# Moving the third layer's expert-weight preparation behind its attention, on four banks, and the fourth layer's weight loads behind the first eight blocks

## What is computed

```python
x = x + _L2_xattn_ref(_layernorm(x), ctx_768, ...)   # one head of 128, 8 batches
x = x + _L2_ffn_ref(_layernorm(x), gate_w, w1, w3, w2)

def _L2_ffn_ref(x, gate_w, w1, w3, w2):              # HIDDEN = 352, 8 experts, TOP_K = 2
    scores = softmax(xf @ gate_w.T)
    expert_weights, expert_indices = top_k(scores, 2)
    ...
    for e in range(8):
        xe = where(flat_idx == e, x_rep, 0.0)
        h = silu(xe @ w1[e].T) * (xe @ w3[e].T)
        y = y + where(flat_idx == e, h @ w2[e].T, 0.0)
```

## Time and profile before

| | us |
|---|---|
| three runs | 1746.24, 1752.26, 1752.90 |
| median | 1752.26 |
| the profiled execution, its own time | 1750.34 |
| its span | 1748.6 |
| between keys/values and token tail of the second layer | 1002.5 to 1024.3 |
| token tail, boundary | 1024.3 to 1057.2 |
| attention of the third layer | 1057.2 to 1128.2 |
| until the first block | 1128.2 to 1144.65 |
| blocks of the third layer | 1144.65 to 1268 |

### The profile page before, as it was taken

One profiled execution on the slowest core, in us unless ns is written; L12 is line 12 of the kernel. 1 busy time (PEld: TensorE's weight loads), 2 busy tenths in 40 slices (PEclk: granted clock), 3 DMA queues, 4 the chain that ended last, 5 costly groups with the idle time before them and its releaser, 6 DMA issues.

```text
span 1748.6 us, 38773 instructions
## 1 busy us (share of the span) xinstructions
PE 1428.4 (82%) x12639; PEld 1092.7 (62%) x12639; DVE 1140.9 (65%) x3004; ACT 808.6 (46%) x1792; POOL 428.2 (24%) x749
## 2 busy tenths in 40 slices
PE   4989999988999778998966836468847988988977
PEld 2667777766666557777745624356635676766765
DVE  4767777776666658888765445633345888878861
ACT  1655555554343256666642223122215666666632
POOL 2000000011100033333222236733341222222221
PEclk9999999998999899999978957589968999999989
DMA  8999000000000030000001120111110000000000
GB/s 232 264 131 83 0 0 0 0 1 1 1 1 0 0 112 5 3 3 6 3 4 43 45 68 7 38 46 45 37 52 1 2 0 0 0 0 0 1 1 25
DMA packets 109760, 55.07 MB, mean 31 GB/s; under 512 B 44593, under 2 KB 102578, under 8 KB 109474
## 3 DMA queue, kind: packets, MB, share of 16 engines
q1 hardware_dynamic: 106146, 46.53, 14.0%
q0 software_dynamic: 3520, 7.31, 1.3%
HBM read 27.09 MB, written 26.74 MB: 31 GB/s over the span
## 4 chain that ended last, share of the span: by engine, by line
PE 58%; DVE 19%; issue 9%; POOL 5%; ACT 4%; SPq 2%; POOLq 1%; DVEq 1%; DMA 1%; ACTq 0%
PE bank L1579 49%; PE bank L1583 10%; DVE PTs L2315 4%; DVE negm L2301 2%; DVE negm L2304 2%; DVE VxF L787 1%; SPq L883 1%; ACT Pm L1419 1%; POOL token_rows_by_expert L1108 1%; ACT PTs L1377 1%; DVE st L2102 1%; POOLq L657 1%; ACT Qz L1377 1%; POOL yn L1315 1%; DVE rk L2465 1%
## 5 line engine op out<-in xcount | busy, mean ns | idle before, releaser
L1419 ACT ACTIVATE Pm<-bank,negm 128x256 f32<-128x256 f32 x784 | 321.6, 472 | 343.6 <-DVE negm L2304 251.5
L1579 PE MATMUL bank<-kT,Qz 64*128 64x256 f32 (+2 forms) x1568 | 305.1, 409 | 9.7 <-ACT Pm L1419 7.2
L1583 PE MATMUL bank<-ident,Pm 128*128 128x128 f32 x1568 | 233.6, 285 | 58.1 <-DVE PTs L2315 54.6
L2315 DVE TENSOR_TENSOR PTs<-bank,PTs 128x512 f16<-128x512 f32 x384 | 251.2, 682 | 33.3 <-ACT PTs L1377 32.2
L1583 PEld LDWEIGHTS bank<-ident,Pm 128*128 128x128 f32 x1568 | 177.7, 144 | 133.0 <-issue 89.0
L1579 PEld LDWEIGHTS bank<-kT,Qz 64*128 64x128 f32 (+1 forms) x1568 | 186.8, 192 | 84.3 <-issue 49.6
L2304 DVE TENSOR_REDUCE negm<-bank 128x2 f32<-128x512 f32 x264 | 176.3, 686 | 79.5 <-PE bank L1579 75.6
L1377 ACT ACTIVATE PTs<-bank 128x512 f16<-128x512 f32 (+1 forms) x388 | 218.3, 603 | 3.4 <-PE bank L1583 3.2
L1579 PEld LDWEIGHTS bank<-VxF,PTs 128*128 128x128 f16 (+1 forms) x4672 | 186.9, 101 | 11.2 <-DVE PTs L2315 2.8
L1579 PE MATMUL bank<-VxF,PTs 128*128 128x65 f16 (+3 forms) x4672 | 191.2, 190 | 1.9 <-DVE PTs L2315 1.9
L1579 PE MATMUL bank<-Qz,R 128*128 128x128 f16 x978 | 92.1, 230 | 23.1 <-ACT Qz L1377 13.9
(11 more groups left out here) (312 smaller groups left out, 2148.8 us busy)
## 6 DMA issues: line engine op xcount, KB each, us to landing
token_rows_by_expert<-trash SPq DMA_DIRECT2D x10, 1782.0 KB, 17.6
Qz<-token_rows_by_expert SPq DMA_DIRECT2D x62, 66.0 KB, 1.8
Qz<-expert_rows_by_token SPq DMA_DIRECT2D x12, 256.0 KB, 3.2
R<-in_L_ffn_ew SPq DMA_DIRECT2D x2, 1024.0 KB, 7.2
R<-in_L_ffn_w SPq DMA_DIRECT2D x1, 2048.0 KB, 9.5
R<-in_L_xattn_Wkv SPq DMA_DIRECT2D x2, 768.0 KB, 6.5
R<-in_L_ffn_w SPq DMA_DIRECT2D x1, 1408.0 KB, 12.0
R<-in_L_xattn_Wq SPq DMA_DIRECT2D x2, 512.0 KB, 3.9
```

Source lines behind the costliest of these rows:

```text
L1419: last = act.activation(Pm[:, k % 4, qt * S:(qt + 1) * S], bank[k % 2][:, qt * S:(qt + 1) * S], ACT.Exp, bias=negm[:, k % 4, qt:qt + 1])
L1579: return pe.matmul(o, l, r, start=start, stop=stop)
L1583: return pe.transpose(o, i, ident[0:n, 0:n])
L2315: dve.tensor_tensor(PTl[:, k % 4, :], bank[2 + k % 2][:, :], PTh[:, k % 4, :], ALU.subtract).then_inc(s.pt[1].sem, 1)
```

## The change

Three things are moved.

- The preparation of the third layer's expert weights leaves `early(ATT[2])`. A new `routed_weights()` on PE, ACT and DVE does the same 20 fills after the third layer's attention: on PE ahead of the first block's transposes, on ACT after the exponentials of the routing weights, on DVE after the block table. The fills use the four banks 0 to 3 in turn instead of banks 6 and 7, so four can be under way.
- SP issues the ten `l3` loads from within the third layer's block rows, after eight blocks' loads and ahead of the ninth.
- What works on those weights follows: `prep3_part(i - 5)` in place of `prep3_part(i)`, POOL's two maxima before block 15's store in place of block 10's, and POOL waits for `prep[2].filled` ahead of its clears.

```diff
+            def last_layer_weights():
+                sp.wait_ge(prep[2].filled, len(PREP2_UP) + len(PREP2))
+                load("l3", L3Wq, a["L3_xattn_Wq"])
+                load("l3", L3Wkv, a["L3_xattn_Wkv"])
...
+                load("l3", Bpr, a["L3_ffn_B_proj"])
...
                 for i in range(nb):
+                    if F.n == 2 and i == RING:
+                        last_layer_weights()
                     at = sp.value_load(rowoff[0:1, i:i + 1], min_val=0, max_val=8 * REGION + 6 * P)
                     if i >= RING:
...
-            sp.wait_ge(prep[2].filled, len(PREP2_UP) + len(PREP2))
-            load("l3", L3Wq, a["L3_xattn_Wq"])
...
                     if F.n == 1 and i == 14:
                         largest(2)
-                    if F.n == 2 and i == 10:
+                    if F.n == 2 and i == 15:
                         pool.wait_ge(vmax3_rows, 1)
...
+                    pool.wait_ge(prep[2].filled, len(PREP2_UP) + len(PREP2))
                     pool.memset(NVflat, 0.0)
...
+                            prep_evac(move, kind, k, bank_of(n)).then_inc(prep[3].act, 1)
+
+            def routed_weights():
+                act.wait_ge(up_scale, 3)
+                for n, (kind, k) in enumerate(PREP2_UP):
+                    need(act, prep[2].filled, n + 1)
+                    w = 512 if k < 5 else 256
+                    move(l2_parts(kind, k * 512, w)[0], bank[n % 4][:, 0:w], upscale[:, 2:3]).then_inc(prep2_high, 1)
+                for n, (kind, k) in enumerate(PREP2, len(PREP2_UP)):
+                    if n % 2 == 0:
+                        need(act, prep[2].filled, n + 1)
+                        prep_evac(move, kind, k, bank[n % 4]).then_inc(prep[2].act, 1)
 
...
                     act.activation(c_e, c_gd, ACT.Exp).then_inc(r.exped.sem, 1)
+                    routed_weights()
...
+            def routed_weights():
+                s, r = att_s[2], prep[2]
+                loaded(pe, "l2f")
+                need(pe, s.exp, ATT[2].nh)
+                need(pe, s.pt[0], ATT[2].nh // 2)
+                need(pe, s.pt[1], ATT[2].nh // 2)
+                nu = len(PREP2_UP)
+                for n, (kind, k) in enumerate(PREP2_UP + PREP2):
+                    if 4 <= n < nu + 4:
+                        pe.wait_ge(prep2_low, n - 3)
+                    elif n >= 4:
+                        pe.wait_ge(r.dve if n % 2 else r.act, (n - nu) // 2 - 1)
+                    prep_fill(kind, k, bank[n % 4]).then_inc(r.filled, 1)
+                need(pe, r.act, len(PREP2) // 2)
+                need(pe, r.dve, len(PREP2) // 2)
...
             def routed_by_token(F):
 
                 s, r = ffn_s[F.n], routed_s[F.n]
+                if F.n == 2:
+                    routed_weights()
...
+                for n, (kind, k) in enumerate(PREP2_UP):
+                    dve.wait_ge(prep2_high, n + 1)
+                    w = 512 if k < 5 else 256
+                    high, low = l2_parts(kind, k * 512, w)
+                    dve.scalar_tensor_tensor(low, bank[n % 4][:, 0:w], upscale[:, 2:3], high,
+                                             ALU.mult, ALU.subtract).then_inc(prep2_low, 1)
+                for n, (kind, k) in enumerate(PREP2, len(PREP2_UP)):
...
+                        need(dve, prep[2].filled, n + 1)
+                        prep_evac(move, kind, k, bank[n % 4]).then_inc(prep[2].dve, 1)
...
                 dve.tensor_tensor(rowoff[:, 0:nb], c_ro[:, 0:nb], step128[:, 0:nb], ALU.add).then_inc(r.table.sem, 1)
+                if F.n == 2:
+                    routed_weights()
...
                     if F.n == 2:
-                        prep3_part(i)
+                        prep3_part(i - 5)
```

More of the change, by code:

```diff
@@ L1387, in early @@
                 attention(A, ("early",))
-                if A.n in prep:
-                    r = prep[A.n]
-                    before = 0
-                    if A.n == 2:
-                        before = len(PREP2_UP)
-                        act.wait_ge(up_scale, 3)
-                        for n, (kind, k) in enumerate(PREP2_UP):
-                            need(act, r.filled, n + 1)
-                            w = 512 if k < 5 else 256
-                            move(l2_parts(kind, k * 512, w)[0], bank_of(n)[:, 0:w],
-                                 upscale[:, 2:3]).then_inc(prep2_high, 1)
-                    for n, (kind, k) in enumerate(PREP2 if A.n == 2 else PREP3):
-                        if n % 2 == 0:
-                            need(act, r.filled, before + n + 1)
-                            prep_evac(move, kind, k, bank_of(n)).then_inc(r.act, 1)
+                if A.n == 3:
+                    for n, (kind, k) in enumerate(PREP3):
+                        if n % 2 == 0:
+                            need(act, prep[3].filled, n + 1)
+                            prep_evac(move, kind, k, bank_of(n)).then_inc(prep[3].act, 1)
[9 more added lines that the diff above has]
+                        prep_evac(move, kind, k, bank[n % 4]).then_inc(prep[2].act, 1)
             def attention(A, early=None):
@@ L1648, in early @@
                 attention(A, ("early",))
-                if A.n in prep:
-                    r = prep[A.n]
+                if A.n == 3:
+                    r = prep[3]
                     need(pe, att_s[A.n].ring.act, (sum(step[0] in FILLS for step in att_early(A)) + 1) // 2)
                     need(pe, att_s[A.n].ring.dve, sum(step[0] in FILLS for step in att_early(A)) // 2)
-                    if A.n == 2:
-                        loaded(pe, "l2f")
-                    if A.n == 2:
-                        for n, (kind, k) in enumerate(PREP2_UP):
-                            if n >= 2:
-                                pe.wait_ge(prep2_low, n - 1)
-                            prep_fill(kind, k, bank_of(n)).then_inc(r.filled, 1)
-                        pe.wait_ge(prep2_low, len(PREP2_UP))
-                    for n, (kind, k) in enumerate(PREP2 if A.n == 2 else PREP3):
+                    for n, (kind, k) in enumerate(PREP3):
                         if n >= 2:
@@ L1877, in ffn_end @@
                 A = ATT[F.n + 1]
-                if A.n not in prep:
+                if A.n != 3:
                     need(pe, att_s[A.n].ring.act, (sum(step[0] in FILLS for step in att_early(A)) + 1) // 2)
@@ L2222, in early @@
                 attention(A, ("early",))
-                if A.n in prep:
-                    evacuate_prep(A)
+                if A.n == 3:
+                    evacuate_prep3()
             def values_scale_and_ones(A):
@@ L2240, in values_scale_and_ones, with routed_weights, evacuate_prep3 @@
                     last.then_inc(ones_set, 1)
-            def evacuate_prep(A):
-                r = prep[A.n]
-                before = 0
-                if A.n == 2:
-                    before = len(PREP2_UP)
-                    for n, (kind, k) in enumerate(PREP2_UP):
-                        dve.wait_ge(prep2_high, n + 1)
-                        w = 512 if k < 5 else 256
-                        high, low = l2_parts(kind, k * 512, w)
-                        dve.scalar_tensor_tensor(low, bank_of(n)[:, 0:w], upscale[:, 2:3], high,
-                                                 ALU.mult, ALU.subtract).then_inc(prep2_low, 1)
-                for n, (kind, k) in enumerate(PREP2 if A.n == 2 else PREP3):
-                    if n % 2:
-                        need(dve, r.filled, before + n + 1)
-                        prep_evac(move, kind, k, bank_of(n)).then_inc(r.dve, 1)
+            def routed_weights():
+                for n, (kind, k) in enumerate(PREP2_UP):
[5 more added lines that the diff above has]
+                for n, (kind, k) in enumerate(PREP2, len(PREP2_UP)):
+                    if n % 2:
+                        need(dve, prep[2].filled, n + 1)
+                        prep_evac(move, kind, k, bank[n % 4]).then_inc(prep[2].dve, 1)
+            def evacuate_prep3():
+                for n, (kind, k) in enumerate(PREP3):
+                    if n % 2:
+                        need(dve, prep[3].filled, n + 1)
+                        prep_evac(move, kind, k, bank_of(n)).then_inc(prep[3].dve, 1)
             def attention(A, early=None):
```

20 lines of the change are left out of this document (9 added, 11 removed).

## The result

The changed kernel took 1731.53 us (median of four runs, 1729.05 to 1736.52) beside 1752.49 us for the kernel before; the ratio is 0.9892, with an interval of 0.9861 to 0.9923. The forecast was 1731, with a range of 1724 to 1739. The profiled execution of the changed kernel is the slowest of its four, 1736.52 us with a span of 1734.8.

The account below looks back on a forecast made before the run. Between the layers no engine was busy throughout and the preparation stood alone; after the attention PE and ACT idled awaiting POOL's scatters. -21.8 + 1.5 - 0.8 = -21.1 from 1750.3 gave 1729.2, as a median 1731 us, range 1724 to 1739.

Parts of the forecast that it names:

- The 21.8 us taken away: Between second and third layer: without the 20 fills DVE goes straight from the last value copy to the token tail, -21.8 us.
- GpSimd's delay moves along: In the token tail: the 6.9 us before POOL's first instruction follows its trigger, so it does not swallow the gain.
- The preparation after the attention, +1.5 us: Between attention and first block: fills end at 1146.2, midway between both clock cases, against 1144.65, adding 1.5 us.
- case of full clock: Preparation after the attention: DVE sets the pace, the end is at 1144.3, before the first block's rows, cost 0.
- case of half clock: Preparation after the attention: PE sets the pace, the end is at 1147.9, 3.3 us late.
- The first blocks' 0.8 us: First blocks' up projections: a PE that has just worked runs them at a higher clock, -0.8 us.
- The loads at no cost: Ten `l3` loads among the block rows: landed by 1165.1, ninth block wanted at about 1167, cost 0.
- rival 1: Preparation after the attention stays at half clock and sticks out: -18.5 us in all, 1734 us; chance 0.17.
- rival 2: Ninth block's rows come late because the ten loads take twice as long: some 7 us, 1738 us; chance 0.06.
- rival 3: The attention's first 26 us stay at clock 0.50, at most 16 us more, 1747 us; chance 0.07.
- rival 4: The clock stays low through the third layer's blocks, 32 us more, 1763 us, slower; chance 0.04.
- rival 5: More than forecast: preparation at cost 0, blocks' 1.0 us back, up to 2 us from the tail, 1727 to 1729; chance 0.06.

Follow-up runs that it names:

- pool_ready: Changed kernel plus one small GpSimd tensor_scalar behind the last scatter of both routed layers, ahead of the wait for statistics: 1714.72 us, ratio 0.9802 to the kernel before.
- two_banks: Changed kernel with the preparation behind the attention on two banks in place of four: 1736.74 us, ratio 0.9918 to the kernel before.
- again: Changed kernel timed a second time, nothing edited: 1726.92 us, ratio 0.9862 to the kernel before.
- bridge: Changed kernel with 12 more transposes on TensorE behind the preparation, into an unread bank: 1728.5 us, ratio 0.9876 to the kernel before.
- bridge_long: Changed kernel with 32 more transposes on TensorE behind the preparation, into an unread bank: 1728.12 us, ratio 0.9875 to the kernel before.
- loads_first: Changed kernel with the ten loads issued ahead of the third layer's block rows, not after eight blocks' loads: 1737.54 us, ratio 0.9922 to the kernel before.
- old_place_four: Kernel before with the preparation and ten loads at their old place, but using four banks: 1741.53 us, ratio 0.9947 to the kernel before.
- pool_done: pool_ready with GpSimd's drain behind the second and third layers' tails replaced by a wait on its last rows and an increment: 1712.11 us, ratio 0.976.

## Why the prediction was right, and what in it was not

- **The 21.8 us taken away** are there: the value copy ends at 1006.09, the tail starts with it. In the two traces of the changed kernel the stage up to the first tail is 21.1 and 22.0 us shorter; they differ by GpSimd's delay, which was 7.7 us in one (1008.8 to 1016.51) and 6.7 in the other (1007.3 to 1014.04).
- **GpSimd's delay moves along**, as said. That it begins when the first instruction of its kind is reached, and can be passed ahead of the wait, pool_ready shows; the prediction said only that it follows its trigger, and took its length as given. It was worth another 12 to 17 us.
- **The preparation after the attention, +1.5 us, was mis-sized; it is 0.** Its last copy ends at 1126.4, 16.1 us behind its first transpose, where I had put the middle between full and half clock at 1146.2 - 1128.1 = 18.1. From the block table to the last copy it is 10.8 us (1115.58 to 1126.42); my case of full clock has 10.9 there, my case of half clock 14.5. Yet the clock was 0.50 until 1121.6 and only then 1.00. The step that failed is that at half clock TensorE sets the pace: DVE began with four filled banks in hand and made its twelve low halves in 8.4 us (1115.50 to 1123.85), where my case of full clock has 7.8. The last eight fills ran at full clock, 2.91 us for 21 of their 24 transposes, so the half-clock price of 6.0 us was not put to the test there; on two banks they took it again (6.03 in two_banks).
- **The first blocks' 0.8 us did not come.** The up projections took 2.10 us each again, and 1.90 and 2.03 in `again`: TensorE, done at 1125.8, stood still for 1.90 us, and one-microsecond stretches show the clock of 1.00 at 1126.6 gone by 1128.6.

```profile
1126.60:1127.60 1.00, 0.00 (x0) 1.00 0.25 62
1127.60:1128.60 1.00, 0.30 (x1) 0.89 0.25 68
1128.60:1129.60 1.00, 0.50 (x2) 0.50 0.30 68
```

  Filling that pause did not hold the clock (bridge), and the term was not well sized either: with the clock up, in bridge_long, the first blocks are some 0.15 us shorter by it, not 0.8 (above). The two errors, +1.5 and -0.8, nearly cancel, so the total of -21.1 was met by some luck: it is -21.0 by the medians of the first timing and -23.8 in the second. bridge and bridge_long, which hardly differ from the changed kernel, have -23.4 and -23.8, so the first timing is the low one; what the gain has beyond the 21.8 us is not explained.
- **The loads at no cost**: the ninth block's transpose waits for nothing. The ten took 7.3 us to issue (1133.66 to 1140.95) and not 6.0, and the ninth block's load goes out 3 us behind the last of them; it lands with time to spare all the same; the blocks' stage is the same within the spread. Rows that are loaded right behind the ten do wait for them (2.2 us in loads_first), a ninth block that is wanted later doesn't.
- **The rivals.** Half clock throughout (rival 1) is what two_banks does, 0.51 over 25.5 us, and it then costs 9.8 us. With four banks the same transposes ran at 1.00 from 1121.6 on, and at 1.00 from the start at the old place. What separates the two cases in the traces is the waits between the transposes. The Trainium skill, TensorE: Matmul & The Clock Gate, PE-mode transpose, has it that transposes don't bring the full clock; these traces don't agree, with 1.00 from 1121.6 in the changed kernel. The late ninth block (rival 2) did not come. The attention (rival 3) kept its clocks, and so did the blocks (rival 4). Of rival 5 the first part came, a preparation at cost 0, and its range of 1727 to 1729 is nearer to the second timing than the forecast; its 2 us for the loads beside the tail had no row behind them, and from the first tail to the end of the attention the two kernels differ by 0.0 and 0.1 us. (The chance of 0.91 for "faster" should have been 0.89, the sum of all cases but 3 and 4.)
- **What the prediction did not separate** is place and banks. It put the whole 21.8 us down to the place; old_place_four shows that 9.2 of them are there without any move.

What stays open: how the transposes and the waits between them set the clock in detail, and why the clock's short falls at 690, 1393 and 1441 us come in most executions and not in all. No run was made for either.

## What to carry to other kernels

A block of work that fits into a pause costs nothing there, but the pause is measured from its own first wait to the first wanted result, and the moved work brings its own chain: give it enough banks that no engine waits for the one behind, and look at which engine is still busy when the pause begins (here DVE with its table). Move with it whatever was queued behind it, and put loads behind the ones that are wanted first: here the issues in the queue cost more (some 7.6 us) than the transfers did (2.2). When a stall only moves along with the work, ask what it is; a delay that begins when an instruction is reached can be passed ahead of the wait by a small instruction of the same kind.

## What the hardware did that I had not expected

- With four banks in place of two, at the same place, the same 68 transposes ran at a granted clock of 1.00 in place of 0.69, and took 11.6 us in place of 21.8.
- The clock's short falls have fixed places in the program, but an execution can miss them. One of the two traces of the kernel before has the clock at 0.59 and 0.57 for 4 us at 1392 and 1440 and takes 2.9 us more from the second tail to the end; the other has neither. Of the twelve traces of all kernels eleven have the fall at 1440, shifted with the work.
- GpSimd's drain at the end of a layer held TensorE up by 1.5 and 4.1 us more than a wait for GpSimd's own last result (3.5 and 6.1 us against 2.0 in pool_done).
